# Modulation rows by loads from a DRAM scratch, and the turned rows of the next batch two steps earlier

## What is computed

```python
mod = (_silu(c) @ wmod).reshape(16, 6, 1, -1)          # one row of 6*128 per batch
sa, ca, ga, sb, cb, gb = (mod[:, k] for k in range(6))
ga = (2 * (ga >= 0) - 1) * jnp.maximum(jnp.abs(ga), 0.25)   # gb likewise
h = _layernorm(x) * (1 + ca) + sa
x = x + ga * attention(h)      # rms norm, 16 heads of 64, rope, window of 32, softmax, w_out
h = _layernorm(x) * (1 + cb) + sb
x = x + gb * ffn(h)            # small attention over the batches, then one of 8 experts per token
```

## Time and profile before

| | |
|---|---|
| median of 3 runs | 1246.53 us (1246.34 to 1251.84) |
| the profiled execution | 1244.12 us |
| its span | 1242.3 us |
| TensorE busy | 1115.6 us, 90% |
| VectorE, ScalarE, GpSimd busy | 961.4, 932.3, 875.3 us |
| granted TensorE clock, mean | 0.947 |
| first stage | up to about 815 us |

### The profile page before, as it was taken

The page is one execution under the profiler, slowest core; times in us unless marked ns, Lnnn a source line. Parts: engine busy times, 40 slices in busy tenths (PEclk is TensorE's granted clock), DMA queues, the critical chain, the costliest instruction groups (busy, mean ns, idle before and its releaser), DMA issues. The chain is left out here.

```text
span 1242.3 us, 49644 instructions
## 1 busy us (share of the span) xinstructions
PE 1115.6 (90%) x17521; PEld 904.2 (73%) x17521; DVE 961.4 (77%) x4159; ACT 932.3 (75%) x3431; POOL 875.3 (70%) x705
## 2 busy tenths in 40 slices
PE   4899999999999999999999999947989983699991
PEld 2687877887777878778777778725777773588881
DVE  6888898888888888988988888635879764277763
ACT  3789988889889899899898898926867651366660
POOL 3777776877777877768778776644567777178885
PEclk9899999999999999999999999969989885799996
DMA  5766666666666666666666667443133124675110
GB/s 170 207 171 150 166 168 147 171 162 156 166 165 158 168 149 169 165 152 166 166 156 166 159 151 189 123 125 133 61 113 119 61 88 152 161 199 149 59 34 24
DMA packets 108404, 177.50 MB, mean 143 GB/s; under 512 B 19310, under 2 KB 61553, under 8 KB 108032
## 3 DMA queue, kind: packets, MB, share of 16 engines
q1 hardware_dynamic: 100320, 155.14, 48.7%
q0 software_dynamic: 6400, 16.82, 3.8%
q10 hardware_dynamic: 1440, 2.36, 0.8%
HBM read 31.86 MB, written 24.68 MB: 46 GB/s over the span
## 5 line engine op out<-in xcount | busy, mean ns | idle before, releaser
L590 POOL TENSOR_TENSOR qk<-mm,sw 128x1024 f32<-128x1024 f32 x128 | 304.6, 2379 | 109.9 <-DMA sw<-mm 109.9
L674 ACT ACTIVATE pr<-sm,mn 128x96 f32<-128x96 f32 x1024 | 368.8, 371 | 0.3 <-DVE mn L490 0.3
L596 POOL TENSOR_TENSOR pr<-pr,ri 128x768 f32<-128x768 f32 x128 | 189.4, 1480 | 75.3 <-DVE ri L515 75.0
L478 DVE TENSOR_TENSOR mm<-bank,cos 128x512 f32<-128x512 f32 x256 | 175.5, 685 | 84.7 <-PE bank L317 81.3
L674 ACT ACTIVATION_READ_ACCUMULATOR pr<-sm,mn 128x1 f32 x1024 | 202.2, 198 | 0.0
L490 DVE CUSTOM_DVE_ANT_0 sm<-bank,msk 128x96 f32<-128x96 f32 x1024 | 191.0, 252 | 3.6 <-PE bank L343 3.6
L479 DVE TENSOR_TENSOR mm<-bank,sin 128x512 f32<-128x512 f32 x256 | 174.2, 681 | 0.0
L368 PE MATMUL bank<-pT,vw 96*64 96x64 f32 x4096 | 147.5, 225 | 0.0
L368 PEld LDWEIGHTS bank<-pT,vw 96*64 96x64 f32 x4096 | 129.8, 138 | 16.3 <-issue 3.3
L665 ACT ACTIVATE pT<-bank 96x512 f32<-96x512 f32 x256 | 137.4, 588 | 0.0
L387 PE MATMUL bank<-ident,pr 128*96 128x128 f32 x1024 | 132.7, 273 | 0.0
(11 more groups left out here) (205 smaller groups left out, 2524.8 us busy)
## 6 DMA issues: line engine op xcount, KB each, us to landing
sw<-mm SPq DMA_DIRECT2D x512, 128.0 KB, 2.3
vw<-vn SPq DMA_DIRECT2D x128, 192.0 KB, 2.6
vw<-vn SPq DMA_DIRECT2D x128, 128.0 KB, 2.3
rr<-sorted_scratch SPq DMA_DIRECT2D x72, 192.5 KB, 2.7
vw<-vn SPq DMA_DIRECT2D x96, 64.0 KB, 2.2
xt<-in_x SPq DMA_DIRECT2D x16, 256.0 KB, 4.0
x_scratch<-x SPq DMA_DIRECT2D x16, 256.0 KB, 2.4
rr<-x_scratch SPq DMA_DIRECT2D x16, 256.0 KB, 3.1
```

What stands on the lines that cost most here:

```text
L478: dve.tensor_tensor(mm[s % 2][:, 0, j, :], PJ[u % 2][:, :], cos[:, :], ALU.mult)
L590: pool.tensor_tensor(qk[i % 2][:, :, 32:], mm[i % 2][:, 0, :, :], sw[i % 2][:, :, :], ALU.add)\
L596: pool.tensor_tensor(t, t, ri[i % 2][:, :].unsqueeze(2).to_broadcast([P, 8, WK]), ALU.mult)\
L674: ins = act.activation(pr[i % 2][:, h, p, :], ms_[i % 2][:, h, p, :], ACT.Exp, scale=-1.0, bias=mn[i % 2][:, h, p:p + 1], accum_out=sums[i ...
```

## The change

Three things:

1. The spreads of batches 2 to 15 and of `modp` are gone from TensorE, their PSUM uses from `plan`, their copies from ScalarE, and the tile `selb` from VectorE. In their place `ms` is stored once to a DRAM scratch (slot 0), each batch's row is loaded with a zero step over the 128 partitions (slots 3, 11, ...), and `modp` comes by eight loads of 16 partitions in slot 121. All these DMAs are on SyncE's queue. GpSimd waits for the load's semaphore instead of ScalarE's.
2. The turning of the next batch's rows stands ahead of the weighted values on TensorE, `x_high` ahead of `oth` on ScalarE, and `x_low` right behind the masked scores on VectorE.
3. Nothing else moves: the slot (r = 6) is the same.

```diff
+    md_d = nc.dram_tensor("mod_scratch", [2, NB, 3 * C], F32).ap()
...
-                if s % G == 3 and s // G + 2 <= NB:
-                    plan.append(("mod", s // G + 2))
...
+                    if s == 0:
+                        sp.wait_ge(s_gt, 12)
+                        sp.dma_start(md_d.rearrange("k b c -> b k c"), ms[:, :, :]).then_inc(s_mp, 16)
+                    if s % G == 3 and s // G + 2 < NB:
+                        b = s // G + 2
+                        sp.wait_ge(s_mp, 16)
+                        sp.dma_start(mod[:, b, :], md_d[0, b:b + 1, :].to_broadcast([P, 3 * C])).then_inc(s_md, 16)
+                    if s == NI - 7:
+                        for r in range(P // NB):
+                            sp.dma_start(modp[r * NB:(r + 1) * NB, :], md_d[1]).then_inc(s_mp, 16)
...
+                    if s < NI and s % G == 6 and s // G + 1 < NB:
+                        to_columns(s // G + 1)
                     i = s - LV
                     if 0 <= i < NI:
                         half = i // 4
...
-                        if s % G == 6 and s // G + 1 < NB:
-                            to_columns(s // G + 1)
-                        if s % G == 3 and s // G + 2 <= NB:
-                            spread(s // G + 2, bank_of(("mod", s // G + 2)))
                         values(s)
...
-                dve.tensor_copy(selb[:, :].rearrange("p (r b) -> p r b", b=NB),
-                                ident[0:NB, 0:NB].unsqueeze(1).to_broadcast([NB, 8, NB])).then_inc(s_sel, 1)
...
+                    if s % G == 6 and s // G + 1 < NB:
+                        x_low(s // G + 1)
                     i = s - LO
...
-                        if r == 6:
-                            x_low(b)
...
-                    pool.wait_ge(s_mev, b + 1)
+                    if b < 2:
+                        pool.wait_ge(s_mev, b + 1)
+                    else:
+                        pool.wait_ge(s_md, 16 * (b - 1))
...
+                    if s % G == 6 and s // G + 1 < NB:
+                        x_high(s // G + 1)
                     i = s - LV
...
-                    if r == 3 and b + 1 <= NB:
-                        mod_out(b + 1)
-                    if r == 6 and b < NB:
-                        x_high(b)
```

More of the change, by code:

```diff
@@ L81, in program @@
         mg = sbt(p1, "mg", [NB, 2, C])
-        selb = sbt(p1, "selb", [NB, P])
         ct = sbt(p1, "ct", [P, NB])
@@ L123, in program @@
         s_gt = sem("a_gt")
-        s_sel = sem("a_sel")
+        s_md = sem("a_md")
+        s_mp = sem("a_mp")
         s_mb = sem("a_mb")
@@ L248, in _ @@
                 sp.wait_ge(s_b1, 16)
+                sp.wait_ge(s_mp, 16 + 16 * (P // NB))
             @blk.tensor
@@ L259, in bank_of @@
                             pe.wait_ge(s_ve, v[1] + 1)
-                        elif v[0] == "mod":
-                            pe.wait_ge(s_mev, v[1] + 1)
                         elif v[0] == "yt":
@@ L275, in spread @@
                 def spread(b, dst):
[L276 to L281, removed]
+                    pe.matmul(dst[:, 0:384], ident[0:NB, b:b + 1].to_broadcast([NB, P]), ms[:, 0, :], start=True, stop=True)\
+                        .then_inc(s_mb, 1)
                 def values(n):
@@ L639, in mod_out @@
                 def mod_out(b):
[L640 to L645, removed]
+                    act.wait_ge(s_mb, b + 1)
+                    act.activation(mod[:, b, :], banks[4 + b][:, 0:384], ACT.Copy).then_inc(s_mev, 1)
                 act.wait_ge(s_ct, 16)
```

## The result

The changed kernel takes 1232.37 us (median of 4 runs, 1231.36 to 1235.51), the one before 1248.47 in the same comparison (4 runs); the ratio is 0.990, with a 95% interval of 0.987 to 0.993. That is 16 us less, where 17.8 were forecast, and 1232.37 lies inside the range of 1223 to 1237. The two profiled executions differ by less: spans of 1242.3 and 1229.5 us, 12.8 apart, and it is against these that the terms have to be held.

The account below looks back on a forecast made before the run. The prediction took TensorE's full list to bound the first stage. Spreads 11.8, turned rows 7.5 and start 0.5, less 2.0 for `modp`, gave 17.8 us less: 1246.5 - 17.8 = 1228.7 us, range 1223 to 1237.

Parts of the forecast that it names:

- What bounds it: First stage: TensorE's list is full, 99.09 of 100 us busy, so a microsecond taken there is one of the kernel.
- Part 1: Slot r = 3: fourteen spreads leave TensorE's list at 0.84 us each, 11.8 us less.
- Part 2: Slot r = 6: wait for `xl` gone, transposes dearer at 0.59 us; 6.34 instead of 6.86, fifteen times, 7.5 us less.
- The first rival: Slot r = 6: ScalarE holds the turned rows back, so moving them gains 0; 10.3 us less, 1236.2; chance 0.15.
- Part 3: SyncE's queue in r = 3: one row load per batch, issue about 0.6 us, covered; costs nothing.
- The third rival: Row loads from one DRAM row delay the next unit's swaps, stalling r = 6 scores; 24.7 us slower, 1271; chance 0.03.
- Part 4: Slots 0 to 5, bound by SyncE's queue: two added issues against the first spread removed; 0.5 us gained.
- Part 5: Slots 121 to 124: eight `modp` loads delay swaps and `qk`, stalling TensorE; 2.0 us lost, ends 0 and 3.8.
- The second stage: After the first stage: same work and order, only earlier; 2 us allowed either way for the granted clock.

Follow-up runs that it names:

- the loads alone: The changed kernel with all three pieces of the turning of rows back in their old places: median 1238.42 us, ratio 0.997 to the kernel before.
- the moved turning alone: The kernel before with only the order of TensorE, ScalarE and VectorE changed for the turned rows, spreads kept: median 1234.89 us, ratio 0.992.
- the early loads: The changed kernel with the store of `ms`, the first row load and the eight `modp` loads issued before the loop: median 1225.02 us, ratio 0.985.

## Why the prediction was right, and where it was off

**What bounds it** was right. What was taken from TensorE's list and from its waits came off the batch: 48.62 to 47.22, where 47.28 was named.

**Part 1, the spreads:** 0.84 us each, as the row said, with the loads alone as with the change. The rule of the Trainium skill quoted there (TensorE: Matmul & The Clock Gate, back-to-back issue gap, with four passes) gives 0.65 as an estimate and would have left the r = 3 slot at 5.94. The slot shows 5.75, so the measurement decides for the row.

**Part 2, the turned rows:** 6.34 forecast, 6.35 measured, with the price of the transposes in the new place (0.59 against 0.58) and the spare of `xl` (0.08 against 0.09) as worked out. Missed were 0.04 us in r = 7: its first product, which came after idle time, took 0.34 us to the start of the next (304.04 to 304.38) and now takes 0.31 (296.60 to 296.91). The first rival, ScalarE holding the rows back, did not happen. `xh` begins 4.89 us after the slot's start (290.26 to 295.15), and `oth`, in whose place it stands, began 4.90 after it (297.18 to 302.08): ScalarE came forward as far as TensorE did. Whether it would have done so with its copy of the spread kept is not shown, since no run took the spread away and left the copy. The run with only TensorE's turning early shows what that rival would have looked like, 6.87 and the releaser `xl`.

**Part 3, the row loads:** nothing, as taken, but for a thinner reason than given. The load lands 1.2 us later than the row I judged it by, and three of them at once cost 36.6 us: the room was there for one. The DMA view of the kernel before has a nearer row, a load of the same 192 KB from DRAM, which the prediction did not use:

```profile
wmod<-in_wmod SPq DMA_DIRECT2D x2, 192.0 KB, 3.9
```

It would have given the 3.8 us to within 0.1. The third rival named the right mechanism and a size that this load does not reach.

**Part 4, the start,** was mis-sized: with the first turning 0.5 + 0.5 less was forecast, and slots 0 to 7 take 0.7 us more (45.70 for 45.04). That slot 8 begins 0.4 earlier is no gain of the change: slot 0 began at 22.27 in the first profile of the kernel before and at 21.17 in its second. The reading of the earlier trace rows was wrong in two places. The 1.50 us of the first spread are those of a low clock, not of its place. The stretch view before, and below it that of the changed kernel, with the granted clock third from the end:

```profile
40.00:45.00 5.00, 4.23 (x16) 2.48 (x9) 4.19 (x22) 1.48 (x6) 4.49 (x3) 0.61 0.66 174
40.00:45.00 5.00, 3.65 (x42) 2.41 (x43) 5.00 (x24) 3.77 (x19) 4.29 (x3) 1.00 0.71 189
```

Where the clock still held at that point, in the profile of the moved turning alone (0.95 from 40 to 42 us), the same spread took 0.91. And the 0.77 us of waiting ahead of it did not go with it; the same wait for `mm` now stands before the values. What the queue does was right, as the early loads show: with the two issues out of it the start is 2.4 us shorter, twice the 1.2 us that the issues take. In this profile they were paid in slot 6 (8.54 us; 6.34 with the early loads), with waits of 1.65 us for `qk` and 0.40 for `mm`.

**Part 5, `modp`, is the term that was most mis-sized:** 4.1 us for 2.0, and beyond its own end of 3.8. The chain was as described, late swap, late `qk`, a wait at the scores of 2.50 us; the 1.3 us that I let faster swap issues give back were only 0.6 (they took 3.14 instead of 3.72). So 0.5 of the 2.1 us missed are in the wait. The other 1.6 are missing from the term altogether: after the wait, TensorE went on at its low level of 1.2 GHz. In the seven profiles with these loads in slot 121, the clock held after waits of 1.98, 2.12 and 2.94 us, and slot 124 grew by 2.04, 2.19 and 3.01; it fell after waits of 2.47, 2.50, 2.72 and 3.02, and the slot grew by 4.07 to 5.91 (after 2.47, by 4.86 and the next slot by 0.8). So a wait of a given length may or may not be followed by it: the two of 2.94 and 3.02 are on either side.

**The second stage** was taken as unchanged, with 2 us either way; it took 3.1 more. Its instructions are the same (6603 products on TensorE in every profile). In ten profiles it runs from 419.9 to 428.3, and it goes with its granted clock: 0.86 in the two of the kernel before, 0.85 in the changed one and the four others up to 424.6, 0.83 or 0.84 in the three from 425.8 on. Both profiles of the kernel before are the shortest, and eight with an altered first stage, one of them with no DMA added, are all longer; on the other chip the kernel before is the longest of four. Whether the change has a part in how the clock falls there, or these are too few, stays open.

By terms: forecast 11.8 + 7.5 + 0.5 - 2.0 = 17.8; in the profiles 19.6 + 0.4 - 4.1 - 3.1 = 12.8. The medians give 16. The terms are thus 5.0 us off: 0.8 better in the batches, 0.6 worse at the start, 2.1 worse at `modp`, 3.1 worse in the second stage. The forecast of the time was only 3.7 off (1232.4 for 1228.7), because the median of the changed kernel's runs lies 1.0 above its profiled execution and not 2.4 as taken from the kernel before. Those 1.4 us are luck.

## What to carry to other kernels

In a stretch where one engine's list is full, price an instruction by the distance between its neighbours' starts at the place where it will stand; such distances were right to 0.02 us here, in both places of the same transposes. A load that replaces compute is free only as far as its issue queue is empty where it is issued, or what stands behind it in the queue has room: ten issues moved to where the queue had nothing to do gave 5.8 us of the first stage. And a short wait on TensorE has two prices, the wait itself and what the clock does after it; bound the second separately (0 to 3.2 us here).

## What the runs showed that was not expected

- After a wait of 2 to 3 us on TensorE in an otherwise full stretch, the granted clock fell in four of seven profiles (0.66 in the 5 us that follow, in the changed kernel), which added 1.6 to 3.2 us to the wait; in three it held, and less than 0.1 was added.
- Loads that read one row of DRAM for all 128 partitions landed in 6.3 us where two such loads were added behind another, and singly in 3.8; added loads of the same size from 128 rows of a weight landed in 4.1 (on another chip).
- Eight loads of 24 KB take 3.7 to 4.6 us of the queue to issue, 0.46 to 0.57 each, about as much each as a load of 192 KB.
